# Layer-1 scores as plain fp32 products in four row groups, with one pool of seven PSUM banks

## The reference

```
# layer 0: single-head attention, then an FFN with blockwise FP4 quantisation
x = x + ga * attn0(h, Wq, Wk, Wv)
x = x + gb * fp4_linear(silu(fp4_linear(h, w_gate)) * fp4_linear(h, w_up), w_down)
# layer 1: 16 heads of width 8, causal
qkv = h @ qkv_kernel + bias;  qkv_heads = qkv.reshape(b, 16, s, 24);  q, k, v = split(qkv_heads)
attn = softmax(q @ k.T / sqrt(256) + causal_mask)      # 256 x 256 for each head
x = x + ga * (attn @ v).reshape(b, s, e)
# layer 1: mixture of 4 usable experts, the 2 best of them weighted by a router, 704 hidden
x = x + gb * sum_e cw[t, e] * (silu(x @ w1[e]) * (x @ w3[e])) @ w2[e]
```

## Time and profile before

| | |
|---|---|
| median of 3 runs | 2192.94 us (2183.0 to 2194.02) |
| profiled execution, its own time | 2209.41 us |
| its span | 2207.7 us |
| PE busy | 2023.7 us, 92% |
| DVE busy | 1552.6 us, 70% |
| ACT busy | 735.9 us, 33% |
| granted TensorE clock, mean | 0.92 |

### The profile page before, as it was taken

The page is one execution under the profiler, slowest core; times in us unless marked ns, Lnnn a source line. Parts: engine busy times, 40 slices in busy tenths (PEclk is TensorE's granted clock), DMA queues, the critical chain, the costliest instruction groups (busy, mean ns, idle before and its releaser), DMA issues.

```text
span 2207.7 us, 36821 instructions
## 1 busy us (share of the span) xinstructions
PE 2023.7 (92%) x12681; PEld 1502.5 (68%) x12681; DVE 1552.6 (70%) x3759; ACT 735.9 (33%) x1447; POOL 68.9 (3%) x78
## 2 busy tenths in 40 slices
PE   1457799999999999999999999999999999999998
PEld 1233567777776767677686767777676777777776
DVE  6356475968777685868868586877868696876464
ACT  0121415242332525243342514344252424333331
POOL 0000000000000000000000000000000000000000
PEclk9865779998997989899899979999897999999899
DMA  4011200203030200303020020303021030202000
GB/s 123 22 40 50 77 20 20 75 10 91 11 91 11 77 20 5 91 11 91 11 87 14 23 68 11 91 11 91 11 63 33 6 91 12 84 12 77 12 13 5
DMA packets 130096, 97.17 MB, mean 44 GB/s; under 512 B 28000, under 2 KB 124512, under 8 KB 125824
## 3 DMA queue, kind: packets, MB, share of 16 engines
q1 hardware_dynamic: 121536, 91.74, 14.5%
q10 hardware_dynamic: 8448, 4.20, 0.7%
HBM read 56.48 MB, written 29.98 MB: 39 GB/s over the span
## 4 chain that ended last, share of the span: by engine, by line
PE 73%; DVE 17%; issue 5%; ACT 2%; DMA 1%; SPq 1%; DVEq 1%; POOL 0%; ACTq 0%; POOLq 0%
PE y_ps L1419 13%; PE b_bank L1315 13%; PE b_bank L1311 5%; PE up_ps L1412 4%; PE gate_ps L1412 4%; PE b_bank L1379 3%; PE a_bank L1170 3%; PE gate_ps L1414 3%; PE gate_ps L1413 3%; PE up_ps L1413 3%; PE up_ps L1414 3%; DVE mneg L1051 3%; PE a_bank L1285 2%; PE b_bank L1170 2%; DVE h L1146 2%
## 5 line engine op out<-in xcount | busy, mean ns | idle before, releaser
L1419 PE MATMUL y_ps<-wd,h 128*128 128x128 f32 (+1 forms) x3072 | 414.0, 284 | 1.3 <-DVE mixed L1133 0.4
L1419 PEld LDWEIGHTS y_ps<-wd,h 128*128 128x128 f32 (+1 forms) x3072 | 382.6, 195 | 44.7 <-issue 20.7
L777 ACT ACTIVATE tt<-gate_ps 128x512 f32<-128x512 f32 x352 | 210.8, 599 | 603.6 <-PE gate_ps L1414 576.3
L1138 DVE SCALAR_TENSOR_TENSOR tt<-tt,gate_ps 128x512 f32<-128x512 f32 x352 | 240.0, 682 | 148.4 <-ACT tt L777 145.3
L1146 DVE TENSOR_TENSOR h<-tt,up_ps 128x512 f32<-128x512 f32 x352 | 239.8, 681 | 85.0 <-PE up_ps L1414 66.9
L737 ACT ACTIVATE arena<-b_bank 128x512 f32<-128x512 f32 x384 | 209.3, 598 | 232.8 <-PE b_bank L1315 232.7
L1051 DVE TENSOR_REDUCE mneg<-b_bank 128x2 f32<-128x512 f32 x256 | 164.6, 684 | 39.6 <-PE b_bank L1315 37.1
L1412 PE MATMUL up_ps<-h_hi,wu_hi 128*128 128x512 f32 x352 | 178.7, 508 | 7.1 <-DVE h L1146 6.0
L1412 PE MATMUL gate_ps<-h_hi,wg_hi 128*128 128x512 f32 x352 | 165.9, 471 | 16.5 <-DVE h_lo L1113 10.1
L1315 PE MATMUL b_bank<-k_stack,q_stack 24*128 24x128 f32 (+1 forms) x1024 | 173.9, 449 | 0.0
L1315 PE MATMUL b_bank<-q_stack,k_stack 26*128 26x256 f32 (+1 forms) x1024 | 173.4, 445 | 0.0
(11 more groups left out here) (189 smaller groups left out, 2933.0 us busy)
## 6 DMA issues: line engine op xcount, KB each, us to landing
q_stack<-q_rows SPq DMA_DIRECT2D x16, 1024.0 KB, 5.4
k_stack<-k_rows SPq DMA_DIRECT2D x16, 1024.0 KB, 7.6
q_rows<-qk_halves SPq DMA_DIRECT2D x48, 256.0 KB, 3.1
k_rows<-qk_halves SPq DMA_DIRECT2D x48, 256.0 KB, 3.7
rows<-mod_rows SPq DMA_DIRECT2D x48, 128.0 KB, 3.2
rows<-mod_rows SPq DMA_DIRECT2D x16, 384.0 KB, 4.8
x_in<-in_L_attn_X SPq DMA_DIRECT2D x16, 256.0 KB, 7.8
vals<-arena SPq DMA_DIRECT2D x128, 32.0 KB, 2.1
```

The costliest lines, as they stand in the source:

```text
L777: send(a(tt[:, ch % 2, :], gate_ps[:], ACT.Tanh, scale=0.5), tanh_ready)
L1138: send(v.scalar_tensor_tensor(tt[:, ch % 2, :], tt[:, ch % 2, :], 1.0, gate_ps[:], ALU.add, ALU.mult), g_free)
L1419: ins = mm(y_ps[:, P * t:P * (t + 1)], h32[rows_, ch % 3, P * t:P * (t + 1)], wd[rows_, ch, :], start=first and t == 0, stop=last_ and t = ...
```

## The change

Scores of layer 1 are made by plain fp32 products on unsplit q and k: 8 contraction rows for `maxima`, 9 for `rows` (8 features and the maximum). The halves, their DRAM copies, and the split of the maxima are gone; `stack` copies 128-column blocks of q32 and k32 within SBUF, four DMAs each, and `stack_max` four. A unit now fills four banks, one for each group of 32 rows, and its products take the groups in turn; there are 6 units of maxima and 6 of rows. The probabilities are kept for three units of four banks (before: four units of two).

All banks but `y_ps` form one pool of seven, and a list `USES` names the bank of every use in a turn, those of gate and up chunks (`eg0`, `eu0`, ...) too. The waits follow from the list. All five orders are new: FIRST is 3, so there are 20 turns; layer-1 projections move to lead 1, the end of the experts (gate 17 and up, down 14 and up) to lead -1.

```diff
-FIRST, LAST = 4, 1
+GROUPS = 4
+HTILE = NHP // GROUPS
+SCORES = ("A0", "B0", "B1", "A1", "B2", "B3")
+TURNED = ("E0", "L0", "E1", "E2", "L1", "E3")
+PROBS = 3 * GROUPS
+FIRST, LAST = 3, 1
+USES = [(-1, "eu15", "D", 3), (1, "T3", "A", 0), (-1, "eu16", "D", 6), ...
...
-        a1_bank, a2_bank = bank("a1_bank"), bank("a2_bank")
-        b_banks = [bank(f"b_bank{i}") for i in range(3)]
-        gate_ps, up_ps, y_ps = bank("gate_ps"), bank("up_ps"), bank("y_ps")
+        pool_banks = [bank(f"bank{i}") for i in range(7)]
+        y_ps = bank("y_ps")
+        ps = Banks(pool_banks, signal)
...
-            def stack(it):
-                sp.wait_ge(halves_stored.sem, halves_stored.at(it, 6))
-                for dst, src in ((q_stack, q_rows), (k_stack, k_rows)):
-                    send(sp.dma_start(dst[:].bitcast(F32), src.rearrange("g r c x -> (g r) c x")), stacked)
+            def stack(it, k):
+                src, dst, use = ((q32, q_stack, "LQ"), (k32, k_stack, "LK"))[k]
+                sp.wait_ge(*ps.is_freed(it, use))
+                for g in range(GROUPS):
+                    send(sp.dma_start(dst[32 * g:32 * g + HD, :, :], src[:, P * g:P * (g + 1)]), stacked)
...
-            def query1(it):
-                own(it, hi1_ready, 1)
-                frees(v.scalar_tensor_tensor(q_lo, ra2.bank("LQ")[:], cols[:, 2:3], q_hi.bitcast(F32), ALU.add, ALU.subtract), ra2, "LQ")
...
             def maxima(it, u):
-                for g in couple(q):
-                    masked(it, use[g], mask_q, by_key(use[g], P) if kind == 0 else by_key(use[g], S)[:, :, P:S], 2 if kind else 4)
+                for g in range(GROUPS):
+                    masked(it, use[g], mask_q, by_key(use[g], S)[:, :, P:S] if wide else by_key(use[g], P), 2 if wide else 4)
                 heads = 2 if wide else 4
                 for j in range(heads):
-                    for g in couple(q):
+                    for g in range(GROUPS):
+                        h = HTILE * g + heads * n + j
+                        if wide:
+                            last = add(ps.bank(use[g])[:, S * j:S * (j + 1)], stack_cols(q_stack, HD, h, 1), stack_both(k_stack, HD, h))
...
             def gate(it, ch):
-                pe.wait_ge(g_free.sem, g_free.at(it, ch) if ch else g_free.before(it, CHUNKS))
-                send(product(gate_ps[:], wg_hi[:, ch, :], wg_lo[:, ch, :]), g_ready)
+                free(it, f"eg{ch}")
+                send(product(ps.bank(f"eg{ch}")[:], wg_hi[:, ch, :], wg_lo[:, ch, :]), ps.signal_ready(f"eg{ch}"))
```

770 lines of the change are left out of this document (380 added, 390 removed), and 30 rows, old and new, of tables (B_USES, USES).

## The result

| | before | after |
|---|---|---|
| median | 2193.48 us (2183.0 to 2194.76, 4 runs) | 2281.6 us (2269.03 to 2290.69, 4 runs) |
| span of the profiled execution | 2207.7 us | 2289.0 us |
| PE busy | 2023.7 us, 92% | 2090.1 us, 91% |
| granted TensorE clock, mean | 0.92 | 0.906 |
| a turn of the loop, mean of ten | 126.8 us | 135.1 us |

The changed kernel is slower: ratio 1.041, 95% interval 1.036 to 1.046. The forecast was 2155 us, and the range ended at 2275.

A forecast was written before the change was run, and what follows sets the result against it. PE's own instructions were taken to set the turn; 1.7 - 1.5 - 2.5 = -2.3 us a turn, 16 turns -37, fill -6, gave 2166 profiled, 2150 by the median, stated as 2155 us; range 2035 to 2275.

The forecast's parts named there:

- Bound by TensorE's own instructions: Whole loop: PE is busy 97% of a turn, so its occupancy, few waits and clock set the time.
- The units: Layer-1 score units: score part 2.04 us for 128 columns and 2.02 for 256; masks 0.95 and 0.55 us.
- The choice of 1.67 ns for a strided fp32 column: Score products' moving operand: each element read twice, 1.67 ns a column, the upper bound; the lower was 0.83.
- rival A: Score products: single reads, strided fp32 stream at 0.83 ns a column, -9.5 us a turn, 2035 us; chance 0.20.
- rival B: Score products: records go in order, row groups no longer overlap; 2500 us, or 2320 with single reads; chance 0.10.
- The net of scores, masks and the first products behind the units: Layer-1 units: 2.9 us a turn more, less 1.2 us of spared exposed weight loads, net +1.7 us.
- exposed weight loads: First product after each score unit waits for its weights: 2.4 us for 24 units; twelve units spare 1.2 us.
- Of 3 us a turn I let half go, -1.5: PE's waits, with the seven-bank pool and new orders: -1.5 us a turn, bounds -3 and +4.
- The signs that the prediction named as its being wrong: Score units and masks: a unit's records do not overlap, or waits at the masks exceed 3 us a turn.
- I take -2.5 of 5.8 us: TensorE's half-clock stretch among maxima units: 2.5 of its 5.8 us a turn go, bounds -5.8 and +4.
- rival C: Dense rows: bank waits or half clock grow, doubling weigh (4 x 1.4 us); +4 us a turn, 2257 us; chance 0.18.
- The fill, -6: Start of the kernel, the transfers in the chain for pair 0: 6 us off the fill, bounds 0 and 15.

The follow-up runs named there:

- one pass: The changed kernel with its score products in fp32r instead of fp32, one record per product: 1985.38 us, ratio 0.906; later variants shorten or move TensorE's loop.
- the moved kernel: The kernel before with 128 instructions (256 waits long met) put ahead of TensorE's loop, nothing in the loop changed: 2184.11 us.

## Why the forecast was wrong

**Bound by TensorE's own instructions: right**, up to a point. Where the scores' 14.3 us were taken out (one pass) the turn lost all of them and 5.0 more, with the clock. But a turn of the loop already costs the changed kernel 3.3 us more than the same turn outside it, and in the one-pass kernels, at 116 us a turn, VectorE's chain is what ends last there.

**The units: right.** 2.04 and 2.03 us measured, 2.04 and 2.02 forecast; their masks 0.96 and 0.54 to 0.64 against 0.95 and 0.55. The choice of 1.67 ns for a strided fp32 column, made between two bounds, holds; rival A (1.2 us a unit) and rival B (over 3.5) are out. The rule behind B, that matmuls run strictly in the program's order, does not hold across row groups here (2.06 us with the groups one after the other), though the run with eight records in a row shows that rival B's mechanism is near. The net of scores, masks and the first products behind the units was forecast at +1.7 us a turn and measured -1.0. (By its own rows the exposed weight loads were 24 x 0.11 = 2.6 us and not 2.4, which moves the sum by 0.1; rival B's 2500 and 2320 were put together less strictly than the forecast.)

**"Of 3 us a turn I let half go, -1.5": this step failed.** Idle time went from 3.3 to 6.5 us a turn, +3.2. At full clock (last column of the table) all steps but the scores take 105.3 us; in the one loop turn of before at full clock it was 121.2 - 21.1 = 100.1. So +5.2 net of what masks and first products gained, against -1.5 forecast; the bound was +4. With the scores' own 3.3 it makes up the turn's 8.4. Two things are in it.

- The loop's branch, which the forecast did not have at all. The turns of the changed kernel just ahead of the loop and just behind it took 130.4 and 130.2 us, those in the loop with the same 13.7 us at half clock 133.5: +3.3, where before had at most 0.8. TensorE stands 1.7 us there and VectorE 2.5. The 1.7 must not be added up as the fetch's cost: in the one-pass kernels the 3.3 to 3.5 us stay when it goes. The forecast read the wait of up to 1.2 us for h_lo as a matter of PE's order; it stands right behind VectorE's stall at its branch, and the new order puts a longer chain (xh, x, h) there.
- Steps that stand alone. The forecast counted only waits, but a step of one or two products by itself pays for its weights and its latency too: projections and transposes cost 3.7 us a turn more, only 2.0 of it idle.

The signs that the prediction named as its being wrong did not come: the records of a unit overlap, and the waits at the masks were 0.5 us a turn. It watched the banks and not the branch.

**"I take -2.5 of 5.8 us" for the clock: mis-sized.** It cost 5.8 before (5.5 measured against the loop turn at full clock) and 5.4 after: -0.4 at most, against -2.5. It changed its place rather than its size. Weigh runs at half clock for 3.4 us a turn where it never did. That is rival C, whose 2257 us came nearest; it expected up to 4 x 1.4 us on weigh, and 1.4 came; its waits for banks did not.

**The fill, -6: mis-sized the other way.** From the first turn_max to the last, fifteen turns, before took 1858.5 us of its span and after 1984.7, +126 or 8.4 a turn. What lies outside fell from 349.2 to 304.3 us. So fill and drain gave 45 us, with one turn fewer to fill and no staging through DRAM; no run parts the two. Together 126 - 45 = 81, the difference of the spans (2289.0 - 2207.7). Had the turn come out as forecast, the kernel would have been at about 2110.

Not settled: why the kernel before loses nothing by fetching its loop (2184 and 2193 us, single runs). Within the moved kernel the stall is not free: the six turns with one took 126.5 us, the other four 122.1. But the half clock was shorter, 7 to 8 us a turn in place of 17, and why that is no run shows.

## What to carry to other kernels

Split a change into its parts before pricing it: here a layout with its order, worth -9%, and a precision worth +15% came in one diff, and the version with fp32r products (1985 us, less accurate) beats both kernels. Price an operand by how its elements lie, since a step of 16 cost 0.9 us a unit here and half as much again as clock for its neighbours. When an order is rewritten, look for small steps that lose the long stream beside them, and take a stall as worth something only after naming what waits right behind it. Compare a turn in the loop with the same turn written out outside it: the difference is the price of the branch, and an order decides what stands there.

## What the runs showed of the hardware

- fp32 products with a moving operand at a step of 16: 1.67 ns a column for each row group, four groups at once. At a step of 2 or 1 the same unit takes 1.13 to 1.16 or 1.08 to 1.10 us in place of 2.04, at full clock; at half clock the units with both operands side by side take 2.02 too.
- Row groups overlap in full with four records of a group issued in a row (2.06 us), and only in part with eight (5.2 in place of 2.04).
- TensorE's loop was kept when it lay in seven pieces of 256 instructions (38 packets in all) and fetched again when it lay in eight: 40 instructions ahead of the loop took 128 packets to 38, 128 others took 38 to 93 (six turns of ten).
- VectorE stood 2.5 us at its loop's branch in the new order and 1.3 in the old one. In the new order a turn in the loop took 3.3 to 3.5 us more than the same turn outside it, with TensorE's loop kept or fetched.
- The clock fell beside strided scores, and near waits of 2 to 4 us where the scores were not strided; with both operands side by side and no wait above 2.1 us all but 1.5 us of a turn ran at full clock. Each us at half clock cost the changed kernel 0.29 us.
- GpSimd took 4.6 us for 2048 fp32 elements a row, for 8 rows as for 128, and a VectorE operation beside it 3.95 us in place of 0.34. SP issued one transfer in 0.65 us.
